# A graph layer with experts: nodes and edges in turned order, narrower edge pairs, and 24 of 25 node tiles beside the edges

## The reference, cut to what matters

```python
xn = _layernorm(x)
W = einsum('rb,bio->rio', comp, basis)                 # 8 relations from 4 bases
msgs = einsum('ni,rio->nro', xn, W)[src, edge_type]
agg = segment_sum(msgs, dst)                           # sum over each node's edges
g = gelu(agg + xn @ loop_w + h_bias + xn)
x = x + layernorm(g) * ln_gamma + ln_beta + mix(xn)    # mix: a softmax over nodes, a 256x256 product, a norm
z = _layernorm(x)
e = argmax(z @ router_w.T + router_b)                  # one of 32 experts for each node
out = x + relu(relu(z @ W1[e] + b1[e]) @ W2[e] + b2[e])
```

## Time and profile before

| | |
|---|---|
| median of 3 runs | 648.89 us |
| the profiled execution | 648.73 us |
| its span, from first to last instruction | 647.0 us |
| granted TensorE clock, mean over the span | 0.948 |
| first and last gather of the edges start | 5.39 and 515.31 us |
| last edge matmuls end | 520.68 us |
| last write of `oh_sum` ends | 544.38 us |

### The profile page before, as it was taken

The page is one execution under the profiler, slowest core; times in us unless marked ns, Lnnn a source line. Parts: engine busy times, 40 slices in busy tenths (PEclk is TensorE's granted clock), DMA queues, the critical chain, the costliest instruction groups (busy, mean ns, idle before and its releaser), DMA issues.

```text
span 647.0 us, 10654 instructions
## 1 busy us (share of the span) xinstructions
PE 543.5 (84%) x3190; PEld 444.8 (69%) x3191; DVE 399.5 (62%) x1372; ACT 200.9 (31%) x406; POOL 443.4 (69%) x465
## 2 busy tenths in 40 slices
PE   0777998998888866899999999998999993289990
PEld 0676997866666665686878787886878762167880
DVE  6868776533343345455776767677566776716883
ACT  4666700000000010215552424242242452045540
POOL 6777777777777777777777777777777700374555
PEclk9969999999999987999999999999999996579996
DMA  8983333333333444334444544454444418464112
GB/s 274 256 251 103 105 101 98 106 98 106 102 106 103 114 155 131 106 98 145 134 140 136 146 133 146 125 151 131 122 150 124 146 46 241 110 198 137 66 66 71
DMA packets 41265, 85.37 MB, mean 132 GB/s; under 512 B 10665, under 2 KB 22890, under 8 KB 41011
## 3 DMA queue, kind: packets, MB, share of 16 engines
q0 software_dynamic: 21968, 61.03, 33.2%
q1 hardware_dynamic: 18372, 22.95, 11.2%
q10 hardware_dynamic: 864, 0.65, 0.3%
HBM read 71.79 MB, written 12.81 MB: 131 GB/s over the span
## 4 chain that ended last, share of the span: by engine, by line
PE 54%; POOL 17%; DMA 10%; DVE 8%; issue 8%; ACT 1%; ACTq 0%; POOLq 0%; DVEq 0%
PE ps L965 21%; POOL acc_raw L583 11%; PE ps L1027 11%; PE ps L1016 6%; DMA gath<-xn_d,src_i 4%; POOL gath L583 4%; PE ps L1233 3%; PE ps L1242 3%; DMA acc_raw<-xn_d,src_i 3%; PE ps L982 3%; DMA both<-rows_d,inv_i 2%; POOL both L669 1%; DVE raw_stats L1343 1%; DMA rel_of<-in_relation_of 1%; PE ps L1050 1%
## 5 line engine op out<-in xcount | busy, mean ns | idle before, releaser
L583 POOL DMA_INDIRECT gath<-xn_d,src_i x200 | 200.5, 1003 | 61.0 <-issue 52.4
L583 POOL DMA_INDIRECT acc_raw<-xn_d,src_i x168 | 164.0, 976 | 51.2 <-issue 43.6
L1400 DVE TENSOR_TENSOR wmat<-hit,wts 128x576 f32<-128x576 f32 x100 | 75.8, 758 | 137.2 <-PE ps L965 137.0
L965 PE MATMUL ps<-wmat,acc_raw 128*128 128x144 f32 x768 | 118.3, 300 | 31.4 <-DMA acc_raw<-xn_d,src_i 20.9
L965 PEld LDWEIGHTS ps<-wmat,acc_raw 128*128 128x128 f32 x768 | 105.7, 197 | 45.9 <-issue 29.0
L965 PE MATMUL ps<-wmat,gath 128*128 128x144 f32 x800 | 122.3, 294 | 6.8 <-DMA gath<-xn_d,src_i 6.6
L1424 DVE TENSOR_TENSOR acc_raw<-acc_raw,ps 128x144 f32 x392 | 100.6, 298 | 36.1 <-PE ps L965 35.1
L965 PEld LDWEIGHTS ps<-wmat,gath 128*128 128x128 f32 x800 | 107.9, 190 | 18.6 <-DMA gath<-xn_d,src_i 9.0
L669 POOL DMA_INDIRECT both<-rows_d,inv_i x25 | 24.1, 964 | 50.9 <-DVE inv_i L1690 42.6
L1027 PE MATMUL ps<-wk_et,acc_raw 128*128 128x256 f32 (+1 forms) x200 | 51.2, 380 | 0.0
L1027 PE MATMUL ps<-wq_wv,acc_raw 128*128 128x256 f32 (+1 forms) x200 | 51.0, 379 | 0.0
(11 more groups left out here) (225 smaller groups left out, 720.9 us busy)
## 6 DMA issues: line engine op xcount, KB each, us to landing
rows_d<-both SPq DMA_DIRECT2D x24, 256.0 KB, 2.2
gath<-xn_d,src_i POOLq DMA_INDIRECT x200, 2.7
both<-in_x SPq DMA_DIRECT2D x24, 128.0 KB
acc_raw<-xn_d,src_i POOLq DMA_INDIRECT x168, 2.8
both<-in_x SPq DMA_DIRECT2D x4, 640.0 KB, 10.6
xn_d<-both SPq DMA_DIRECT2D x4, 640.0 KB
acc_raw<-in_w_t SPq DMA_DIRECT2D x1, 2080.0 KB
acc_raw<-in_w_t SPq DMA_DIRECT2D x1, 2048.0 KB, 7.4
```

The lines of the kernel that those rows point to most:

```text
L583: g.indirect_dma_start(place_of(n), None, table, bass.IndirectOffsetOnAxis(ap=src_i[:, n:n + 1], axis=0)).then_inc(done, 16)
L965: ins = t_.matmul(ps_edge[quarter][:, m * B * WIN:(m + 1) * B * WIN], place_of(n)[:, m * P:(m + 1) * P], wmat[:, k, :, :].rearrange("p b w ...
L1400: d.tensor_tensor(wmat[:, half * w:half * w + w, :, :], hit[:, :, :].unsqueeze(2).to_broadcast([P, w, B, WIN]), wts[:, :, cut].rearrange(" ...
```

## The change: turned order, two widths of pairs, and 24 tiles in the loop

The host hands over `x` and the edge lists in reversed order, so the nodes with few edges come first and the dense ones last. The sources and destinations still hold the old numbers: DVE turns `src_i` into `N - 1 - src` at the start, before the first gather (`pool.wait_ge(src_loaded, 17)`), columns are counted from the greatest old number of a pair (`high` is stored instead of `low`, and `rel` is that less `dst`), the base row is turned once, and the output's row numbers are turned in `out_i`. Pairs from octet 26 on are 20 columns wide instead of 36 (`width`), in `hit`, `wmat`, the matmuls and the adds; `judge` checks both widths. All octets from 25 to 48 start a node tile, so that tiles 0 to 23 go through the loop; `early` of tile 24 stands in octet 48 before the last quarter's edges and uses the bank `ps_mix[0]`. As more nodes are reached in the first octets, the 32 slots in `acc` are used up to octet 15 only (`EARLY = 16`), six tiles are cleared at the start, one in each of octets 2 to 11, and tiles 16 to 24 in octets 16 and 17.

```diff
-WIN = 36
+WIN, SLIM = 36, 20
+NARROW = 26
-STARTS = [25, 26, 27, 28, 29, 30, 31, 32, 33, 34, 35, 36, 37, 38, 39, 40, 42, 43, 44, 45, 46, 47, 48]
+STARTS = list(range(25, 49))
-EARLY = 24
+EARLY = 16
-NEAR, MIDDLE = 8, 33
-CLEAR = {0: 2, NEAR: HIGH, MIDDLE: NT}
+FIRST_CLEAR = 6
+NEAR, MIDDLE = HIGH - 2, EARLY + 2
+def width(q):
+    return WIN if q < NARROW else SLIM
...
-            return ps_edge[0] if t == NT - 1 else ps_mix[t % 2]
+            return ps_mix[t % 2]
...
-            pool.wait_ge(src_loaded, 16)
+            pool.wait_ge(src_loaded, 17)
...
-            for t in range(CLEAR[0]):
+            for t in range(FIRST_CLEAR):
                 clear_tile(t)
...
-                if 2 + 2 * q < HIGH:
-                    clear_tile(2 + 2 * q)
-                    clear_tile(3 + 2 * q)
+                if q + 1 >= RAW and q + 4 < HIGH:
+                    clear_tile(q + 4)
...
-                    if q == EARLY + 1:
-                        act.wait_ge(multiplied, (EARLY + 1) * OCT)
-                    for t in range(HIGH + 2 * (q - EARLY - 1), min(HIGH + 2 * (q - EARLY), NT)):
-                        clear_tile(t)
...
+                    if q == EARLY:
+                        act.wait_ge(multiplied, (EARLY + 1) * OCT)
+                    if q >= EARLY:
+                        for t in range(HIGH + 5 * (q - EARLY), min(HIGH + 5 * (q - EARLY) + 5, NT)):
+                            clear_tile(t)
...
-                        ins = t_.matmul(ps_edge[quarter][:, m * B * WIN:(m + 1) * B * WIN], place_of(n)[:, m * P:(m + 1) * P],
-                                        wmat[:, k, :, :].rearrange("p b w -> p (b w)"), start=k == pair[0], stop=k == pair[-1])
+                        w = B * width(q)
+                        ins = t_.matmul(ps_edge[quarter][:, m * w:(m + 1) * w], place_of(n)[:, m * P:(m + 1) * P],
+                                        wmat_tiles[:, k, 0:w], start=k == pair[0], stop=k == pair[-1])
...
+                if q == NOCT - 1 and quarter == 2:
+                    early(NT - 1, once)
                 if t is not None and quarter == 3:
                     product(t, 5, KD * B, once)
-                if q == NOCT - 1 and quarter == 3:
-                    early(NT - 2, once)
...
-            product(NT - 2, 0, KD * B, once)
-            logits(NT - 5, once)
-            turn_row(NT - 4, once)
-            early(NT - 1, once)
             product(NT - 1, 0, B, once)
             logits(NT - 4, once)
             turn_row(NT - 3, once)
...
+            v.wait_ge(src_loaded, 16)
+            d.tensor_scalar(src_i[:, :], src_i[:, :], -1.0, float(N - 1), ALU.mult, ALU.add).then_inc(src_loaded, 1)
...
-            finish_row(NT - 4, once)
-            first_stats(NT - 3, once)
-            second_stats(NT - 3, once)
             finish_row(NT - 3, once)
-            route(NT - 5, once)
             first_stats(NT - 2, once)
...
+                at = o.mark(d.tensor_scalar(out_i[:, :], inv_i[:, :], -1.0, float(N - 1), ALU.mult, ALU.add))
...
+    arrays["x"] = np.ascontiguousarray(arrays["x"][::-1])
+    src = np.pad(arrays.pop("src")[::-1], (0, pad)).reshape(ETAB, P)
+    types = np.pad(arrays.pop("edge_type_8")[::-1], (0, pad), constant_values=R).reshape(ETAB, P)
+    dst = np.pad(arrays.pop("dst")[::-1], (0, pad), mode="edge").reshape(ETAB, P)
```

## The result

The changed kernel takes 642.49 us (median of 5 runs, 642.01 to 644.07); the kernel before, in the same runs, 648.89. The ratio is 0.9913, with an interval of 0.9891 to 0.9936: 0.9% faster. The forecast, 639.4, was 3.1 us too low; the range, 635 to 646, holds the time. Medians here leave out single executions in which the chip was disturbed. The profiled execution took 642.49 us (span 640.69; before 648.73 and 646.99), so the span is 6.3 us shorter.

The account below looks back on a forecast made before the run. TensorE was taken to bound the chain octets (10.51 us), with the gathers only 0.45 us behind. Terms: -6.4 + 2.1 + 0.2 - 5.2 = -9.3, so 648.7 becomes 639.4 us; its own range 636.5 to 642.5, the wider one 635 to 646.

Parts of the forecast that it names:

- Narrow pairs: Octets 26 to 48: 80 instead of 144 columns, matmul records 0.111 us apart by weight loads, octet 10.51 to 10.15: -6.4 us.
- Rival (a): Octets 26 to 48: TensorE falls well below the gathers' pace, octets run at 10.06 us; -13.5, 635.2 us; chance 0.15.
- (b): Octets 26 to 48: the narrower pairs bring nothing, octets stay at 10.51 us; -1.1, 647.6 us; chance 0.12.
- One more tile: Tile 23 moves from tail into octet 48: `early` of tile 24 delays the last edges 2.1 us, tail gives 5.2.
- The wait for the copy of tile 22: Tail: tile 22's logits wait for ACT's copy of its turned row, done 9.5 us after the last edges.
- Gather slots: Octets 16 to 23, 8 slots instead of 32: 1.9 us to spare, so 0; up to 2 us if small products stall longer.
- Start: First gather waits until DVE has turned `src_i`: delay 0 to 0.6 us, taken as 0.2, counting in full; clears hidden.
- The rest stays: After the last `oh_sum` (544.38 us): edges, gathers, products and expert pairs as many as before, so no change there.
- Rival (c): GpSimd in octets 26 to 48: DVE builds hold more gathers, octets 10.86 us; +7.0, 655.7 us; chance 0.06.

## Why the prediction was nearly right, and where it failed

1. *Narrow pairs* (-6.4). Right, in mechanism and size: octets 26 to 48 take (507.47 - 275.81)/183 x 8 = 10.13 us by the gathers (10.15 forecast, 10.43 before, 10.41 with wide pairs), 6.9 us less from the first of these gathers to the last. Matmul records with 80 columns start 0.112 us apart (the median of 519 gaps within quarters from 310 to 500 us; 0.111 forecast from the logits' weight loads), those with 144 columns in the trace of before 0.123. Rival (a), 0.068 from the columns, and (b), no gain, have both fallen. The Trainium skill, page TensorE: Matmul & The Clock Gate, section LDWEIGHTS, gives a weight load of 128 columns 107 ns; the trace's 112 is 5% above it. So the octet, at 10.12 us, stays 0.06 above the gathers' 10.06, and did not fall to the 10.0 that was estimated from the page's figure.
2. *One more tile* (+2.1, -5.2). From the last gather's start to the last edges' end it took 8.16 us instead of 5.37, 2.8 more (2.1 forecast). The tail was 19.1 us, 18.5 forecast, so it gave 4.6. The wait for the copy of tile 22 came where it was named (3.55 us), and moving the copy took most of it away. Of the missing 0.6 some 0.4 lies in a length that the forecast took from another clock: the logits of tile 22 took 0.63 us in the earlier trace rows at a granted clock of 1.00, and 1.06 after that wait, at 0.50 (1.2 GHz, the lower level), which TensorE was granted from 524.65 on.
3. *Gather slots* (0). **The step that failed.** Its reason held: octet 26 begins in time, at 275.81 us here and at 276.68 in the kernel before with this edit alone (276.76 without). But I priced the edit only in the octets where it works. It costs 3.67 us at the very end, in GpSimd's closing drain.
4. *Start* (+0.2). The first gather comes 0.13 later.
5. *The rest stays.* From the last `oh_sum` to the last scatter it did (96.06 us, before 96.39). "What follows 544.38 stays" took in the end of the program without a look at what fills it. The row stood in the trace of before: a drain of 9.00 us, 4.74 of it behind the last work. The Trainium skill, page VectorE: DVE Perf Modes, section The DRAIN you can't avoid, puts the drains of a program's preamble and postamble at a constant 12 ns or so on all five engines. Whether it means the drains at the end of this kernel's block, it does not say; there SyncE's took 7 ns, ScalarE's 798 and GpSimd's 12,370, so its figure is no price for GpSimd's.

The sum: -9.63 to the last `oh_sum`, -0.33 to the last scatter, +3.66 to the end: -6.30, the difference of the spans. That -9.63 lies so near the forecast of -9.3 is partly luck. The tile gave 1.8 net instead of 3.1; the narrow pairs gave 6.9 instead of 6.4, and octet 26 begins 0.95 us earlier where +0.2 was forecast. This last is within what executions differ by: in the six traces of the kernel before and its variants the first gather of that octet starts between 274.89 and 277.04.

Rival (c) did not come. In the kernel before 17 gathers of octets 26 to 48 last over 1.25 us; each starts inside a build of `wmat` and ends 0.82 us after it. They are gone with the shorter builds (none of the changed kernel lasts over 1.3 us from octet 16 on), and with wide pairs 16 are back (up to 1.38).

## What to carry to other kernels

Read the last rows of a trace as a stage of its own: between the last useful instruction and the end of the span there can be several microseconds, and an edit far away can change them. Where an engine has idle time ahead of a point that it must pass anyway, do the closing work there: one added instruction was worth 3.8 us here, though in the kernel before it shortened the closing drain by 0.58 us only. The narrower matmul was worth only what its weight loads left (0.011 of the 0.054 us that the columns promise). A length read at one granted clock does not hold at the other: the logits behind the long wait in the tail took 1.06 us instead of 0.63.

## What the runs showed of the hardware that was not expected

GpSimd's drain takes 0.19 us at the start of the program. At the end it lasts 4.7 to 8.4 us beyond the last issue behind 442 indirect DMAs (8.40 where all data had landed before it began), 4.16 behind 50, 2.38 behind 25 scatters, 1.73 behind 9, and 3.30 behind 25 row gathers. The closing drain's length is the same to 0.01 us in the profiled executions of programs that issue their indirect DMAs alike, and it changes with which gathers go to which slots. The drain behind the last edge gather varies more in the three kernels of the changed order that have it (6.05, 6.53 and 6.26 us), but in all three it ends 2.5 us after the last data have landed.
